# Value products of the first attention in two 64-column tiles, transposes and value products further behind the scores, six probability buffers

## The reference

```
x = x + g_msa * attention(modulate(layernorm(x), sh_msa, sc_msa))
    q, k, v = split(x @ W_qkv)              # 16 heads of 64
    attn = softmax(q @ k^T * 64**-0.5)      # 256 x 256 for each head and sequence
    out  = (attn @ v) @ W_out + b_out
x = x + g_mlp * mlp(...)                    # gelu MLP, 512 wide
# layer 2: rotary attention, 16 heads of 8, and a gated MLP
# layer 3: quantised linear layers with a gated scan, and an MLP
# layer 4: linear attention over 16 heads of 8
```

## Time and profile before

| what | value |
|---|---|
| median of 3 runs | 571.14 us (568.64 to 576.99) |
| span of the profiled execution | 575.8 us |
| first attention on PE | 21.9 us (scores of pair 0) to 214.5 us (end of the last `result`) |
| PE busy over the span | 445.2 us, 77% |
| DVE, ACT, POOL busy | 376.4, 320.5, 193.6 us |

### The profile page before, as it was taken

The page is one execution under the profiler, slowest core; times in us unless marked ns, Lnnn a source line. Parts: engine busy times, 40 slices in busy tenths (PEclk is TensorE's granted clock), DMA queues, the critical chain, the costliest instruction groups (busy, mean ns, idle before and its releaser), DMA issues.

```text
span 575.8 us, 8155 instructions
## 1 busy us (share of the span) xinstructions
PE 445.2 (77%) x2640; PEld 344.1 (60%) x2641; DVE 376.4 (65%) x904; ACT 320.5 (56%) x989; POOL 193.6 (34%) x189
## 2 busy tenths in 40 slices
PE   5889999999999976855799899889997252064574
PEld 5567677677677754634799789879454141013354
DVE  3355547546566624495988699787228919979884
ACT  1564553663564628578578878755442573174252
POOL 1044332433344412001739468110561203353101
PEclk9999999999999997998789899999679565555587
DMA  8920000000000000000000000000000000000001
GB/s 323 442 89 2 0 1 1 1 2 2 0 2 1 1 1 1 1 0 1 1 2 1 1 2 1 2 2 1 0 0 2 1 0 0 0 3 0 0 2 36
DMA packets 3842, 13.33 MB, mean 23 GB/s; under 512 B 372, under 2 KB 2420, under 8 KB 3284
## 3 DMA queue, kind: packets, MB, share of 16 engines
q1 hardware_dynamic: 3800, 12.80, 5.6%
HBM read 12.28 MB, written 0.52 MB: 22 GB/s over the span
## 4 chain that ended last, share of the span: by engine, by line
PE 53%; DVE 23%; ACT 11%; issue 7%; POOL 4%; DMA 1%; POOLq 0%; SPq 0%; ACTq 0%; DVEq 0%
PE bank L954 8%; PE bank L883 6%; PE bank L906 6%; PE bank L926 4%; ACT big L483 4%; PE bank L940 4%; POOL big L392 3%; DVE area L1311 3%; PE bank L1019 3%; PE bank L911 3%; PE bank L968 3%; PE bank L869 2%; DVE area L1314 2%; DVE tab_ L1311 2%; PE bank L1165 2%
## 5 line engine op out<-in xcount | busy, mean ns | idle before, releaser
L392 POOL TENSOR_TENSOR big<-big,rrec 128x512 f32<-128x512 f32 x64 | 65.2, 1039 | 119.9 <-DVE rrec L1505 119.9
L483 ACT ACTIVATE tab_<-bank,nmax 128x256 f32<-128x256 f32 x128 | 59.2, 467 | 32.5 <-DVE nmax L1455 30.5
L883 PE MATMUL bank<-vpad,xT 128*128 128x96 f32 x512 | 71.2, 285 | 7.6 <-DVE xT L1461 7.4
L483 ACT ACTIVATE big<-bank,nmax 128x256 f32<-128x256 f32 x128 | 59.0, 472 | 24.0 <-PE bank L906 13.6
L883 PEld LDWEIGHTS bank<-vpad,xT 128*128 128x128 f32 x512 | 65.5, 200 | 11.5 <-DVE xT L1461 10.5
L483 ACT ACTIVATE area<-bank 128x512 f32<-128x512 f32 (+3 forms) x68 | 37.1, 550 | 60.4 <-PE bank L911 18.5
L1489 DVE TENSOR_REDUCE nmax<-bank 128x2 f32<-128x512 f32 x64 | 41.7, 685 | 36.8 <-PE bank L926 36.8
L954 PE MATMUL bank<-area 128*128 128x256 f32 x256 | 60.6, 380 | 0.9 <-ACT big L483 0.9
L483 ACT ACTIVATE big<-bank 64x256 f32<-64x256 f32 (+1 forms) x73 | 29.5, 405 | 47.6 <-PE bank L954 35.9
L1497 DVE COPY area<-bank 128x512 f32<-128x512 f32 x64 | 42.8, 686 | 17.8 <-PE bank L940 17.8
L1455 DVE TENSOR_REDUCE nmax<-bank 128x2 f32<-128x512 f32 x64 | 43.5, 680 | 12.0 <-PE bank L860 11.7
(11 more groups left out here) (221 smaller groups left out, 909.5 us busy)
## 6 DMA issues: line engine op xcount, KB each, us to landing
w2s<-w SPq DMA_DIRECT2D x1, 4352.0 KB, 26.5
rows<-row SPq DMA_DIRECT2D x1, 1600.0 KB, 10.9
w0s<-w SPq DMA_DIRECT2D x3, 512.0 KB, 6.9
w1s<-w SPq DMA_DIRECT2D x1, 1408.0 KB, 15.8
w0s<-w SPq DMA_DIRECT2D x1, 1024.0 KB, 12.9
xs<-x SPq DMA_DIRECT2D x1, 512.0 KB, 4.3
out<-tab_ SPq DMA_DIRECT2D x2, 256.0 KB, 2.3
tabs<-tab SPq DMA_DIRECT2D x1, 421.5 KB, 5.3
```

The source lines that it names most:

```text
L392: pool.tensor_tensor(prob[:, n % 4], prob[:, n % 4], rrec0[:, n % 4, :].unsqueeze(2).to_broadcast([P, QT, SEQ]), ALU.mult).then_inc(S("a0_ ...
L483: return nc.scalar.activation(o, i, f, **kw)
L883: m = mm(bank[4 + gslot][:, o:o + v(k).shape[1]], A.pT[:, half, k, q * P:(q + 1) * P], v(k), start=(k == 0), stop=(k == QT - 1))
```

## The change

Four things are done together.

1. `pair_values` computes for each head only its own 64 value columns. The weights are `vs[..., c*P + a*64 : c*P + (a+1)*64]` and the product of head a goes to partitions a*64 to a*64+63 of the same 256 columns of `bank[6]`. The two heads alternate inside the loop over key tiles. `take_outputs0` is then one copy of 128 x 256 and not two of 64 x 256.
2. TURN_LAG = 2, VALUE_LAG = 3: transposes of pair s - 2 and value products of pair s - 3 stand in step s. `result`, `batch_out` and `batch_normed` move one step later, and so does the step without units (UNIT_STEP), with the two waits that follow from that.
3. Six probability buffers and not four: two more lie in `ta` (a part of `tab_`).
4. On DVE `worth0(s - 1)` stands in step s behind the first `top0`, where `worth0(s)` stood at the end of step s.

```
-        UNIT_STEP = [(0, 1), (2, 3), (), (4, 5), (6, 7), (8, 9), (10,), (11,)]
+        UNIT_STEP = [(0, 1), (2, 3), (4, 5), (), (6, 7), (8, 9), (10,), (11,)]
+        SLOTS = 6
+        TURN_LAG, VALUE_LAG = 2, 3
...
             def exponents(n):
-                if n >= 4:
-                    act.wait_ge(S("a0_T"), n - 3)
+                if n >= SLOTS:
+                    act.wait_ge(S("a0_T"), n - SLOTS + 1)
...
             def take_outputs0(p):
-                for a in range(2):
-                    r = slice(a * DH0, (a + 1) * DH0)
-                    m = acti(aT[r, p % 8, :], bank[6][r, a * SEQ:(a + 1) * SEQ], ACT.Copy)
-                m.then_inc(S("a0_aT"), 1)
+                acti(aT[:, p % 8, :], bank[6][:, 0:SEQ], ACT.Copy).then_inc(S("a0_aT"), 1)
...
             def pair_values(p):
-                for a in range(2):
-                    for k in range(QT):
-                        n = 2 * p + a
-                        m = mm(bank[6][:, a * SEQ:(a + 1) * SEQ], vs[:, b % 2, k, c * P:(c + 1) * P],
-                               pT[:, n % 4, k, :], start=(k == 0), stop=(k == QT - 1))
+                for k in range(QT):
+                    for a in range(2):
+                        m = mm(bank[6][a * DH0:(a + 1) * DH0, 0:SEQ],
+                               vs[:, b % 2, k, c * P + a * DH0:c * P + (a + 1) * DH0],
+                               pT[:, (2 * p + a) % 4, k, :], start=(k == 0), stop=(k == QT - 1))
...
-            for s in range(PAIRS + 3):
+            for s in range(PAIRS + VALUE_LAG + 1):
+                turned_pair = s - TURN_LAG if TURN_LAG <= s < PAIRS + TURN_LAG else None
-                if 1 <= s <= PAIRS:
-                    turn0(2 * s - 2)
+                if turned_pair is not None:
+                    turn0(2 * turned_pair)
...
-                if s % 8 == 2 and s > 8:
+                if s % 8 == VALUE_LAG and s > 8:
                     result(s // 8 - 1)
-                if 2 <= s < PAIRS + 2:
-                    pair_values(s - 2)
+                if VALUE_LAG <= s < PAIRS + VALUE_LAG:
+                    pair_values(s - VALUE_LAG)
...
                 if s < PAIRS:
                     top0(2 * s)
+                if 1 <= s <= PAIRS:
+                    worth0(s - 1)
...
-                if s < PAIRS:
-                    worth0(s)
```

More of the change, by code:

```diff
@@ L179, in cond_seq_kernel @@
         prob, aT = views(big[:, :], (4, QT * SEQ), (8 * SEQ,))
+        more, = views(ta.rearrange("p t d -> p (t d)"), (2, QT * SEQ))
         qT, kT = (v.rearrange("p s (c k) -> p s c k", c=8) for v in (qT, kT))
         vs = vs.rearrange("p s (k d) -> p s k d", k=QT)
-        pT, prob = (v.rearrange("p s (k q) -> p s k q", k=QT) for v in (pT, prob))
+        pT, prob, more = (v.rearrange("p s (k q) -> p s k q", k=QT) for v in (pT, prob, more))
+        prob = [prob[:, n] for n in range(4)] + [more[:, n] for n in range(2)]
         aT = aT.rearrange("p (c q) -> p c q", c=8)
@@ L391, in normalised @@
                 for n in (2 * p, 2 * p + 1):
-                    pool.tensor_tensor(prob[:, n % 4], prob[:, n % 4],
+                    pool.tensor_tensor(prob[n % SLOTS], prob[n % SLOTS],
                                        rrec0[:, n % 4, :].unsqueeze(2).to_broadcast([P, QT, SEQ]), ALU.mult
@@ L533, in exponents @@
                 act.wait_ge(S("a0_max"), n + 1)
-                if n >= 4:
-                    act.wait_ge(S("a0_T"), n - 3)
+                if n >= SLOTS:
+                    act.wait_ge(S("a0_T"), n - SLOTS + 1)
                 for q in range(QT):
-                    e = acti(prob[:, n % 4, q, :], bank[n % 4][:, q * SEQ:(q + 1) * SEQ], ACT.Exp,
+                    e = acti(prob[n % SLOTS][:, q, :], bank[n % 4][:, q * SEQ:(q + 1) * SEQ], ACT.Exp,
                              bias=nmax0[:, n % 4, q:q + 1], accum_out=rsum0[:, n % 4, q:q + 1])
@@ L543, in take_outputs0 @@
                 act.wait_ge(S("a0_PV"), p + 1)
-                for a in range(2):
-                    r = slice(a * DH0, (a + 1) * DH0)
-                    m = acti(aT[r, p % 8, :], bank[6][r, a * SEQ:(a + 1) * SEQ], ACT.Copy)
-                m.then_inc(S("a0_aT"), 1)
+                acti(aT[:, p % 8, :], bank[6][:, 0:SEQ], ACT.Copy).then_inc(S("a0_aT"), 1)
             for u in range(4):
                 take_unit(u)
-            for s in range(PAIRS + 2):
+            for s in range(PAIRS + VALUE_LAG):
                 units = step_units(s)
@@ L562, in _ @@
                     take_unit(i)
-                if s >= 2:
-                    take_outputs0(s - 2)
+                if s >= VALUE_LAG:
+                    take_outputs0(s - VALUE_LAG)
             def weight_sums(names, into):
@@ L898, in unit @@
                     pe.wait_ge(S(unit_taken(i - 4 if i < 8 else i - 1)[0]), unit_taken(i - 4 if i < 8 else i - 1)[1])
-                if j == 4 and b >= 2:
+                if j == 6 and b >= 2:
                     pe.wait_ge(S("a0_y"), b - 1)
@@ L940, in turn0 @@
                         m = nc.tensor.transpose(bank[4 + n % 2][:, k * SEQ + q * P:k * SEQ + (q + 1) * P],
-                                                prob[:, n % 4, q, k * P:(k + 1) * P], ident)
+                                                prob[n % SLOTS][:, q, k * P:(k + 1) * P], ident)
                 m.then_inc(S("a0_T"), 1)
@@ L963, in result @@
                     pe.wait_ge(S("a0_y"), b)
-                before = min((b + 2) * UNITS + 3, NB * UNITS - 1)
+                before = min((b + 2) * UNITS + 5, NB * UNITS - 1)
                 pe.wait_ge(S(unit_taken(before)[0]), unit_taken(before)[1])
@@ L979, in _ @@
                     unit(i)
-                if 1 <= s <= PAIRS:
-                    turn0(2 * s - 2)
+                if turned_pair is not None:
+                    turn0(2 * turned_pair)
                 for i in units[1:2]:
                     unit(i)
-                if 1 <= s <= PAIRS:
-                    turn0(2 * s - 1)
+                if turned_pair is not None:
+                    turn0(2 * turned_pair + 1)
                 for i in units[2:]:
                     unit(i)
-                if s % 8 == 2 and s > 8:
+                if s % 8 == VALUE_LAG and s > 8:
                     result(s // 8 - 1)
-                if 2 <= s < PAIRS + 2:
-                    pair_values(s - 2)
+                if VALUE_LAG <= s < PAIRS + VALUE_LAG:
+                    pair_values(s - VALUE_LAG)
             pe.wait_ge(S("w1_in"), 16)
@@ L1541, in _ @@
                     top0(2 * s + 1)
-                if 1 <= s <= PAIRS:
-                    take0(2 * s - 2)
+                if turned_pair is not None:
+                    take0(2 * turned_pair)
                 for i in units[1:2]:
                     take_keys(i)
-                if 1 <= s <= PAIRS:
-                    take0(2 * s - 1)
+                if turned_pair is not None:
+                    take0(2 * turned_pair + 1)
                 for i in units[2:]:
                     take_keys(i)
-                if s < PAIRS:
-                    worth0(s)
-                if s % 8 == 2 and s > 8:
+                if s % 8 == VALUE_LAG and s > 8:
                     batch_out(s // 8 - 1)
-                if s % 8 == 3 and s > 8:
+                if s % 8 == VALUE_LAG + 1 and s > 8:
                     batch_normed(s // 8 - 1)
```

## The result

The changed kernel takes 542.22 us (median of 4 runs, 538.68 to 545.34), the one before 569.89 us in the same number of runs (568.61 to 576.99). The ratio is 0.949, with a 95% interval of 0.941 to 0.957: 27.7 us less by the medians, where 26.5 were forecast.

A forecast was written before the change was run, and what follows sets the result against it. PE's own queue was taken to bound steps with units, waiting for POOL the last eight. Terms -13.7 - 1.3 - 1.8 - 0.8 - 7.3 - 1.6 = -26.5 us took 571.1 to 544.6 us, range 537 to 560.

The forecast's parts named there:

- The bound: Attention stage: PE's own queue in steps with units; in the last eight steps, PE waiting for POOL's multiplications.
- e: Change in what the value products cost PE in one step, forecast -0.65 us from the row of the scores.
- the second rival: Value products: weight loads stand bare between column tiles, slower than before; e = +0.9, 591 us, chance 0.05.
- Which steps get e: Scores of step 3 to those of step 24, where PE sets the pace: 21e = -13.7 us.
- 30e - 7.0: Whole forecast sum in us as a function of e: 21 + 7 steps and two value products behind the last scores.
- The start: Steps 1 and 2: lag removes a wait for POOL, -1.3 us, and moves value products to the end, -1.8.
- The waits ahead of `result`: Two steps with `result` behind s = 8 and 16: eight transposes 1.42 us against 1.04, -0.4 each, -0.8 us.
- The last eight steps: Steps without units: with the lag 3.27 us each, not 4.31, including 0.15 allowed for DVE; seven steps, -7.3 us.
- Behind the last scores: Last scores to `result`: last value products 0.65 shorter each, copy 0.3 shorter, later reciprocals take back 0.2; -1.6 us.
- the moved work: Value products the lag moves from the start to behind the last scores; absorbed while PE waits for the last pair.
- Buffers and copies: Six probability buffers: nothing; one copy per pair saves ACT 0.3 us per step, nothing in steps with units.
- From the span to the median: Profiled span 575.8 to about 549 us; same 26.5 us taken off the median of 571.1, giving 544.6.

The follow-up runs named there:

- tiles alone: Kernel before with only the value products in two 64-column tiles and one copy per pair; lags, buffers, DVE order as before: 554.15 us, ratio 0.973 to before.
- the lag alone: Changed kernel with the old 128-column value products and two copies of 64 x 256 per pair: 564.80 us, ratio 0.987 to before.

## Why the prediction was right, and where it was off

**The bound** was read rightly: PE's own queue in the steps with units, and the loop over POOL in those without.

**e.** Forecast -0.65 by the row of the scores, measured -0.72. Records of column tiles run side by side as those of row tiles do. The value products take 1.02 us to the next scores where the scores themselves take 1.07: their second pair of records starts 0.27 behind the first and not 0.32. The way in costs 0.09, where 0.10 was assumed. So 1.17 was 1.11.

The rule of the Trainium skill that was weighed against the change (TensorE: Matmul & The Clock Gate, Part 3, The mechanism: weight loads overlap with matmuls in flight only where the row group differs) isn't borne out here: both column tiles use all rows and eight loads are hidden in 1.02 us. The bare loads of the second rival, 591 us, didn't occur.

**Which steps get e.** 21 steps, forecast -13.7 and -0.8 for the result steps, measured -15.7: the same step count with the larger e (21 x 0.72 = 15.1) and 0.6 for the two waits. What the prediction treated as a plain product needs the lag, though. With tiles alone the same stretch gains 12.35. (The start of step 24, put at about 148, would have been 147.1 by the prediction's own terms; it is at 145.66.) The formula 30e - 7.0 held wherever the lag was there: at the measured e = -0.72 it gives -28.6 for -29.5, at e = +0.15 (both heads in one column tile) -2.5 for -2.7, at e = 0 (the lag alone) -7.0 for -6.0. It isn't a sum of two independent parts: the tiles alone give 17.8, not 20 to 22.

**The start** (-3.1 against -3.0) came out as worked out. **The waits ahead of `result`** were somewhat overrated, -0.4 each: from the start of the eight transposes to `result` it was 1.25 us before (82.03 to 83.28) and is 0.93 in the run with the lag alone (173.15 to 174.08), so -0.3. The prediction had compared the lengths of the groups, 1.42 and 1.04, and added up 1.04 from pieces.

**The last eight steps**: forecast 3.27 each, with 0.15 allowed for DVE, measured 3.10. The allowance wasn't needed. -7.3 became -8.5.

**Behind the last scores**: -1.6 forecast, -2.35 measured. The forecast has two parts, and the rows of the changed kernel, to be read against the last three of the earlier trace rows, tell them apart:

```profile
177.74 1.08 PE L954 MATMUL bank<-area 128*64 128x256 f32 x8
179.40 1.08 PE L954 MATMUL bank<-area 128*64 128x256 f32 x8 [0.57 <-ACT big L487]
181.00 3.81 PE L969 MATMUL bank<-w0s,big 128*128 128x128 f32 x32 [0.52 <-issue]
```

That the moved work would be absorbed held: from the last scores to the last value products but one it is 6.79 us (170.95 to 177.74), 6.69 before. It holds only with short value products. With long ones the lag alone costs 1.1 there: that way takes 7.75 us. The mis-sized term is the last two value products with their copies. From the first of them to `result` it is 3.26 us, 5.71 before, so -2.45. Each group is 0.81 shorter by its length (1.89 to 1.08), not 0.65, and each of the two copies 0.39 (0.77 to 0.38), not 0.3. Nor do the prediction's own terms give 1.6: two times 0.65, less 0.2, and 0.3 for one copy make 1.4, for both 1.7.

**Buffers and copies**: "nothing", and four buffers give the same steps. What the shorter copies bring they bring at the end, as just said.

**From the span to the median** the prediction took the same difference off. It could, because the term was one of a stage at full clock. The spans themselves would have misled: the profiled execution of before had lost 8 us to the clock in the second layer. The difference of the stage, 29.5, lies inside the interval of the ratio, which is 24.5 to 33.6 us. That the medians (27.7) come nearer to the forecast of 26.5 than the stage does is luck: every stretch behind step 3 was forecast too small, the stage by 3.0 us in all, and the median lies between two groups of run times.

## What to carry to other kernels

If two heads of 64 share a matmul of 128 weight columns and half of each product is thrown away, put each head's own 64 columns in a column tile of its own: the pair then costs little more than one did (1.02 us here, where both took 1.82). Before shortening the longest queue, look at what it waits for where it is short already: here a step with `result` gained nothing from the tiles alone, since PE then waited for POOL, and a lag of one more pair, which costs nothing but order, was worth twice what it brought by itself (11.7 us on top of the tiles, 6.0 alone). And where PE waits for a bank to be emptied, move work that needs another bank into that wait; here it gave 7 us for lines moved on two engines.

## What the runs showed of the hardware that was not expected

- Two column tiles run side by side in fp32, with both tiles writing one bank on different partitions, and **which of the two orders the program has doesn't matter**: heads alternating or one after the other give 1.02 us for the eight records. In one and the same column tile they take 1.87.
- Changing the tiling costs about 0.1 us on the way in, into column tiles (0.53 for 0.44 from the transposes) as into row tiles: from the last value record to the scores 0.31 from the whole array and 0.32 from column tiles (56.08 to 56.40), where records of one tiling stand 0.215 apart. The change pays one more of these per step.
- A weight load of 64 columns takes 136 ns on average, one of 128 columns took 190: less than in proportion. The group of the changed kernel:

```profile
L954 PEld LDWEIGHTS bank<-area 128*64 128x64 f32 x256 | 15.6, 136 | 10.6 <-issue 4.5 <-DVE area L1499 1.2
```

- The granted clock of the second layer's MLP is 2.4 GHz in some executions and 1.2 GHz in others of the same instructions, and makes 8.0 us of difference. Before the change the fall comes at 407 to 408 us (0.82 there, 0.50 from 408 on), and PE is busy without a gap from 403.86 on, through the fall and to the end of the MLP; its last pause ahead of that, 0.63 us, is there with the same length in the changed kernel, where the clock stays full. Of nine profiled executions six had the long form (33.1 us), two the short one (25.1), and one lay between (29.7). Why an execution gets the one or the other is open, and no run was made for it.
